# Layer 1 selects 11 columns of edges in even blocks and 10 in odd ones

## The reference

```
layer 0: ew  = (edge_attr @ W_e + b_e) as 16 x 16;  msg = x[src] . ew
         x   = layernorm(x + mean of msg over each node's edges + bias)
layer 1: A   = edge_emb[edge_type] as 16 x 16;      msg = A . x[src]
         m   = sum of msg over each node's edges
         x   = layernorm(x + GRU(m, x))
```

## Time and profile before

| what | us |
|---|---|
| median of 3 runs | 4953.85 (4951.73 to 4953.85) |
| the profiled execution | 4951.33 |
| its span | 4949.5 |
| PE busy | 4801.9 (97%) |
| DVE, ACT, POOL busy | 4057.1, 4048.1, 3499.9 |

### The profile page before, as it was taken

How to read it: one execution, slowest core, us unless ns; L and a number is a source line. 1 busy time by engine, 2 the same in 40 slices (tenths; PEclk the granted TensorE clock), 3 DMA queues, 4 the chain that set the end, 5 groups by cost and what they waited for, 6 DMA issues and landing times.

```text
span 4949.5 us, 133716 instructions
## 1 busy us (share of the span) xinstructions
PE 4801.9 (97%) x40480; PEld 4330.9 (88%) x40481; DVE 4057.1 (82%) x5504; ACT 4048.1 (82%) x5764; POOL 3499.9 (71%) x3682
## 2 busy tenths in 40 slices
PE   6999999999999999999979999999999999999997
PEld 5888888888888888888869999999999999999997
DVE  8888888888888888888867777777777777777776
ACT  7888888888888888888658888888888888888885
POOL 7777777777777777777666767676767676767674
PEclk9999999999999999999989999999999999999999
DMA  3221221221111211112221111111111111111111
GB/s 75 35 37 34 37 35 35 37 34 35 37 34 35 37 34 35 37 34 35 33 34 28 27 28 27 28 27 28 27 28 27 28 27 28 27 28 27 28 27 16
DMA packets 371461, 159.41 MB, mean 32 GB/s; under 512 B 232707, under 2 KB 370531, under 8 KB 371291
## 3 DMA queue, kind: packets, MB, share of 16 engines
q1 hardware_dynamic: 254584, 127.93, 11.4%
q0 software_dynamic: 116672, 30.10, 7.8%
q10 hardware_dynamic: 160, 0.80, 0.1%
HBM read 155.84 MB, written 2.66 MB: 32 GB/s over the span
## 4 chain that ended last, share of the span: by engine, by line
PE 84%; DVE 10%; issue 4%; DVEq 1%; POOL 1%; DMA 0%; ACT 0%; SPq 0%; POOLq 0%; ACTq 0%
PE psN L703 66%; PE psM L733 13%; DVE z L900 4%; DVE cand L871 4%; PE psTR L724 1%; PE psTR L728 1%; PE psTR L725 1%; DVE z L875 1%; PE psTR L713 1%; POOL z L461 1%; DVE grp_hot L862 0%; PE psTR L717 0%; PE psTR L714 0%; DVEq L874 0%; PE psN L816 0%
## 5 line engine op out<-in xcount | busy, mean ns | idle before, releaser
L703 PE MATMUL psN<-table_hi,pick 128*128 128x320 f32 (+1 forms) x13020 | 3879.7, 315 | 45.9 <-DVEq L843 31.2
L703 PE MATMUL psN<-table_lo,pick 128*128 128x320 f32 (+1 forms) x13020 | 3769.9, 305 | 0.0
L703 PEld LDWEIGHTS psN<-table_hi,pick 128*128 128x128 f32 x13020 | 2447.5, 188 | 224.4 <-issue 171.9
L703 PEld LDWEIGHTS psN<-table_lo,pick 128*128 128x128 f32 x13020 | 2450.2, 188 | 0.0
L461 POOL DMA_INDIRECT z<-in_x,idx x1885 | 1798.6, 954 | 658.2 <-issue 471.4
L461 POOL DMA_INDIRECT z<-h_rows,idx x1761 | 1682.9, 956 | 708.5 <-issue 475.9
L520 ACT ACTIVATE dist<-src_mod,neg_node 128x640 bf16<-128x640 uint16 (+1 forms) x2480 | 2000.0, 844 | 64.8 <-ACT pick L528 54.8
L528 ACT ACTIVATE pick<-dist,one 128x640 fp32r<-128x640 bf16 (+1 forms) x2480 | 2003.9, 846 | 23.0 <-PE psN L703 6.8
L900 DVE TENSOR_TENSOR z<-psD,z 128x2048 f32<-128x2048 f32 (+1 forms) x750 | 1367.4, 1823 | 102.2 <-issue 57.9
L871 DVE TENSOR_TENSOR cand<-psN,grp_hot 128x640 f32<-128x640 f32 x1364 | 1075.8, 789 | 434.4 <-PE psN L703 364.8
L875 DVE TENSOR_REDUCE z<-cand 128x32 f32<-128x640 f32 x1364 | 1077.6, 790 | 132.0
(11 more groups left out here) (107 smaller groups left out, 681.4 us busy)
## 6 DMA issues: line engine op xcount, KB each, us to landing
src_mod<-src_mod_rows SPq DMA_DIRECT2D x372, 160.0 KB
z<-in_x,idx POOLq DMA_INDIRECT x1885, 2.3
z<-h_rows,idx POOLq DMA_INDIRECT x1761, 2.3
eab<-in_edge_attr SPq DMA_DIRECT2D x125, 200.0 KB
src_mod<-src_mod_rows SPq DMA_DIRECT2D x124, 192.0 KB
idx<-in_src SPq DMA_DIRECT2D x250, 12.5 KB
dstb<-in_dst SPq DMA_DIRECT2D x250, 14.0 KB
grp<-src_grp SPq DMA_DIRECT2D x248, 5.5 KB, 1.6
```

Source lines behind the costliest of these rows:

```text
L703: mm = pe.matmul(rows[:, :, 0:cells.shape[2]], pick[j][:, c, at:at + P], cells, start=(i == 0 and part == 0), stop=(i == TC - 1 and part = ...
```

## The change

`H`, the number of picked columns, gets an entry for each layer and each parity: layer 0 keeps 10 and 10, layer 1 gets 11 in even and 10 in odd blocks, so odd blocks of layer 1 gather 15 columns (column 20 is the one that moves). All that hangs on `H` becomes a table by layer and parity: the halves of ScalarE's work (`HCUT`), the pairs of the selects, the waits of the gathers on picks, and the counts that semaphores are waited for, which are now sums over both parities (`ahead`, `picked_of`, `cand_of`). `TURN`, `RING`, the sizes of buffers and the host's layout stay.

```diff
-H = (10, 11)
-HM = max(H)
+H = ((10, 10), (11, 10))
+HM = max(max(h) for h in H)
-HCUT = ((0, 5, 10), (0, 5, 11))
+HCUT = [[(0, 5, h) for h in hs] for hs in H]
 TURN = (10, 12)
 RING = 4
-FIRST_S = (8, 11)
+FIRST_S = (8, 10)
-AFTER_OWN = ({3: 0, 5: 1, 6: 2, 7: 3, 8: 4, 12: 5, 13: 6}, {5: 0, 6: 1, 9: 2, 10: 3, 11: 4, 12: 5})
-AFTER_LAST = ({1: 8, 2: 9}, {1: 7, 2: 8, 3: 9, 4: 10})
+AFTER_OWN = ([{3: 0, 5: 1, 6: 2, 7: 3, 8: 4, 12: 5, 13: 6}] * 2, [{5: 0, 6: 1, 9: 2, 10: 3, 11: 4, 12: 5}, {5: 0, 6: 1, 9: 2, 10: 3, 11: 4, 13: 5}])
+AFTER_LAST = ([{1: 8, 2: 9}] * 2, [{1: 7, 2: 8, 3: 9}, {1: 7, 2: 8, 3: 9, 4: 10}])
...
+        def ahead(k, buf, r):
+            return sum(H[k]) * r + buf * H[k][0]
+        def picked_of(k, buf, r, n):
+            return ahead(k, buf, r) + H[k][1] + n
+        def cand_of(k, buf, r, n):
+            return ahead(k, buf, r) + RING + n
...
-                def held(t):
-                    if t >= RING:
-                        return t - RING
-                    return max(u for u in range(H[k]) if (u - t - TURN[k]) % RING == 0) - H[k]
-                def pick_rows(b, buf, t):
+                def pick_rows(b, buf, r, t):
...
-                    pe.wait_ge(l["cand"], RING + H[k] * b + held(t) + 1)
+                    if t >= RING:
+                        pe.wait_ge(l["cand"], cand_of(k, buf, r, t - RING + 1))
+                    else:
+                        last = max(u for u in range(H[k][1 - buf]) if (u - t - TURN[k]) % RING == 0)
+                        pe.wait_ge(l["cand"], cand_of(k, 1 - buf, r - 1 + buf, last + 1))
...
-                    for t in range(H[k]):
+                    for t in range(H[k][1 - buf]):
                         if more1:
-                            pick_rows(b + 1, 1 - buf, t)
+                            pick_rows(b + 1, 1 - buf, r + buf, t)
```

More of the change, by code:

```diff
@@ L21 @@
 PICKED = [4, 5, 6, 7, 13, 14, 21, 22, 23, 24, 20]
-H = (10, 11)
-HM = max(H)
-SCUT = [[sum(p < START[j] for p in PICKED[:h]) for j in range(NS + 1)] for h in H]
-HCUT = ((0, 5, 10), (0, 5, 11))
+H = ((10, 10), (11, 10))
+HM = max(max(h) for h in H)
+SCUT = [[[sum(p < START[j] for p in PICKED[:h]) for j in range(NS + 1)] for h in hs] for hs in H]
+HCUT = [[(0, 5, h) for h in hs] for hs in H]
 NH = 2
@@ L29 @@
 FILL = 24
-FIRST_S = (8, 11)
+FIRST_S = (8, 10)
 S_AT, T_AT, R_AT = (4, 1), (5, 3), (6, 5)
-GATHERED = [[[g for g in range(START[j], START[j + 1]) if g not in PICKED[:h]] for j in range(NS)] for h in H]
-assert all(c[-1] == h for c, h in zip(HCUT, H)) and all(2 * n % RING == 0 and n >= h for n, h in zip(TURN, H))
-PAIRS = tuple(tuple((t, min(t + 2, h)) for t in range(0, h, 2)) for h in H)
-AFTER_OWN = ({3: 0, 5: 1, 6: 2, 7: 3, 8: 4, 12: 5, 13: 6}, {5: 0, 6: 1, 9: 2, 10: 3, 11: 4, 12: 5})
-AFTER_LAST = ({1: 8, 2: 9}, {1: 7, 2: 8, 3: 9, 4: 10})
+GATHERED = [[[[g for g in range(START[j], START[j + 1]) if g not in PICKED[:h]] for j in range(NS)] for h in hs] for hs in H]
+assert all(2 * n % RING == 0 and n >= max(hs) for n, hs in zip(TURN, H))
+PAIRS = [[[(t, min(t + 2, h)) for t in range(0, h, 2)] for h in hs] for hs in H]
+AFTER_OWN = ([{3: 0, 5: 1, 6: 2, 7: 3, 8: 4, 12: 5, 13: 6}] * 2, [{5: 0, 6: 1, 9: 2, 10: 3, 11: 4, 12: 5}, {5: 0, 6: 1, 9: 2, 10: 3, 11: 4, 13: 5}])
+AFTER_LAST = ([{1: 8, 2: 9}] * 2, [{1: 7, 2: 8, 3: 9}, {1: 7, 2: 8, 3: 9, 4: 10}])
 SUB = 4
@@ L113, in build @@
         src_mod = [sb(f"src_mod{b}", [P, HM * P], U16) for b in range(2)]
-        HALF = [max(c[j + 1] - c[j] for c in HCUT) for j in range(NH)]
+        HALF = [max(c[j + 1] - c[j] for cs in HCUT for c in cs) for j in range(NH)]
         pick = [sb(f"pick{j}", [P, TC, HALF[j] * P], F32R) for j in range(NH)]
@@ L451, in body @@
                     for j in range(NS):
-                        for g in range(START[j], START[j + 1]) if whole else GATHERED[k][j]:
+                        for g in range(START[j], START[j + 1]) if whole else GATHERED[k][buf][j]:
                             if not whole:
-                                if n in AFTER_OWN[k]:
-                                    pool.wait_ge(l["picked"], H[k] * (b + 1) + AFTER_OWN[k][n] + 1)
+                                if n in AFTER_OWN[k][buf]:
+                                    pool.wait_ge(l["picked"], picked_of(k, buf, r, AFTER_OWN[k][buf][n] + 1))
                                     pool.sem_inc(s_turn)
-                                if n in AFTER_LAST[k]:
-                                    pool.wait_ge(l["picked"], H[k] * b + AFTER_LAST[k][n] + 1)
+                                if n in AFTER_LAST[k][buf]:
+                                    pool.wait_ge(l["picked"], picked_of(k, 1 - buf, r - 1 + buf, AFTER_LAST[k][buf][n] + 1))
                                     pool.sem_inc(s_turn)
@@ L684, in bank @@
                     return (TURN[k] * buf + t) % RING
-                def held(t):
+                def pick_rows(b, buf, r, t):
+                    j = max(j for j in range(NH) if HCUT[k][buf][j] <= t)
+                    at = (t - HCUT[k][buf][j]) * P
                     if t >= RING:
-                        return t - RING
-                    return max(u for u in range(H[k]) if (u - t - TURN[k]) % RING == 0) - H[k]
-                def pick_rows(b, buf, t):
-                    j = max(j for j in range(NH) if HCUT[k][j] <= t)
-                    at = (t - HCUT[k][j]) * P
-                    pe.wait_ge(l["cand"], RING + H[k] * b + held(t) + 1)
+                        pe.wait_ge(l["cand"], cand_of(k, buf, r, t - RING + 1))
+                    else:
+                        last = max(u for u in range(H[k][1 - buf]) if (u - t - TURN[k]) % RING == 0)
+                        pe.wait_ge(l["cand"], cand_of(k, 1 - buf, r - 1 + buf, last + 1))
                     for i, c in enumerate(CHUNKS):
@@ L737, in keep_busy @@
                 def keep_busy():
-                    pe.wait_ge(l["cand"], RING + H[k] * NB)
+                    pe.wait_ge(l["cand"], cand_of(k, 0, (NB - 1) // 2, H[k][0]))
                     for i in range(FILL):
@@ L760, in first_body @@
                     sum_block(0)
-                    for t in range(FIRST_S[k], H[k]):
-                        pick_rows(1, 1, t)
+                    for t in range(FIRST_S[k], H[k][1]):
+                        pick_rows(1, 1, 0, t)
                     flush_transposes(first)
@@ L873, in select @@
                         grp_hot[:, t0:t1, :].unsqueeze(2).to_broadcast([P, m, F, NG]), ALU.mult).then_inc(l["cand"], m)
-                    dve.wait_ge(l["cand"], H[k] * b + t1 + RING)
+                    dve.wait_ge(l["cand"], cand_of(k, buf, r, t1))
                     dve.tensor_reduce(xs[k][buf][:, z_pos[0]:z_pos[-1] + 1:step_pos, :], cand[:, a:a + m],
@@ L897, in outer @@
                     dve.wait_ge(l["got"][buf][j], got_of(k, buf, j, r))
-                    dve.wait_ge(l["sel"], H[k] * b + SCUT[k][j + 1])
+                    dve.wait_ge(l["sel"], ahead(k, buf, r) + SCUT[k][buf][j + 1])
                     dve.wait_ge(l["coef"], b + 1)
@@ L928, in selects @@
                         for n in pairs:
-                            select(1, 1, *PAIRS[k][n])
+                            select(1, 1, 0, *PAIRS[k][1][n])
                     if k == 0:
@@ L950, in first_body @@
                     dve.sem_inc(l["match_x"], 1)
-                    selects(*(range(2, len(PAIRS[k])) if k == 0 else range(5, len(PAIRS[k]))))
+                    selects(*range(2 if k == 0 else 5, len(PAIRS[k][1])))
                     match_block(1, 1, 0)
@@ L968, in selects @@
                             for n in pairs:
-                                select(*nxt[:2], *PAIRS[k][n])
+                                select(*nxt, *PAIRS[k][1 - buf][n])
                     outer(b, buf, r, 2)
@@ L987, in body @@
                         outer(*nxt, 1)
-                    selects(*range(3, len(PAIRS[k])))
+                    selects(*range(3, len(PAIRS[k][1 - buf])))
                     if more2:
@@ L1008, in _ @@
                 dve.sem_inc(l["free"], 1)
-                dve.sem_inc(l["picked"], 2 * H[k])
+                dve.sem_inc(l["picked"], picked_of(k, 1, 0, 0))
                 dve.sem_inc(l["pick_act"], TC * NH + 1)
-                dve.sem_inc(l["cand"], RING + H[k])
-                dve.sem_inc(l["sel"], H[k])
+                dve.sem_inc(l["cand"], cand_of(k, 1, 0, 0))
+                dve.sem_inc(l["sel"], ahead(k, 1, 0))
                 dve.sem_inc(l["hot_g"], 1)
```

18 lines of the change are left out of this document (9 added, 9 removed).

## The result

| | us |
|---|---|
| before, median of 5 runs | 4953.85 (4951.73 to 4954.96) |
| changed, median of 5 runs | 4927.37 (4925.39 to 4930.19) |
| ratio | 0.9947, 95% interval 0.9935 to 0.9958 |
| changed, the profiled execution and its span | 4930.19 and 4928.4 |

The change saves 26.5 us; 4925 was forecast, with 29.2 us. The profiled execution is the longest of the five, so the steady part is read by intervals and not by the span. Its span is 21.1 us shorter than before. From the first to the last sums of layer 1 it is 26.1 us shorter (2335.3 for 2361.3); the rest, 3.7 us ahead of the first sums and 1.2 us behind the last ones, went the other way.

What follows compares the result with a forecast made beforehand. Layer 1 was taken as nearly TensorE-bound, with VectorE's product 2 last by 0.39 us before the sums. 61 x 0.50 = 30.5, less 1.3, gives 29.2 us: 4953.85 - 29.2 = 4924.7, said as 4925; range 4908 to 4944.

Steps and rivals of the forecast that it cites:

- The ring takes the pick back: Pick 0 after an odd block still waits for `cand` of columns 8 and 9; TensorE idles 1.2 to 1.4 us.
- 0.39 us a pair from the sums that no longer wait: At the end of each even body, sums start right after pick 1, no longer after product 2: 0.39 us.
- 0.11 us from ScalarE's shorter half: Odd blocks' second half has 5 columns, not 6, so pick 5 and VectorE's chain come 0.11 us earlier.
- The gather costs nothing in the steady part: GpSimd's 15th gather in odd blocks fills its wait for a buffer: cost 0, at most 2 us in all.
- 1.3 us at the start: Block 1 of layer 1: its 15th gather delays S(1), the start of its sums, costing 1.3 us.
- the third rival: Longer idling lowers TensorE's clock from 2.4 to 1.2 GHz: 5187, or 5010 with only the sums slow; 4%.
- the pauses: Between GpSimd's gathers, 1.6 to 2.0 us over the usual gap; 0.5 us a pair added to its load.
- rival 1: The ring's wait costs nothing and VectorE stays last before the sums: gain 61.5 us, 4892; 6%.

Runs made afterwards that it cites:

- the gather alone: Kernel before, with one gather more in each odd block of layer 1 into a spare buffer, which product 2 waits for: 4955.8 us, 1.0005.
- the skipped banks: Changed kernel, but in odd blocks of layer 1 picks 2 to 9 take the bank two further on: 4892.3 us, 0.9876 of before.
- the cut at 6: Changed kernel with the skipped banks, and the 11 columns of even blocks cut 6 and 5 instead of 5 and 6: 4883.6 us, 0.9860 of before.
- the moved mask and the skipped banks: Changed kernel with the skipped banks, and VectorE's mask made behind product 2 instead of ahead of it: 4877.9 us, 0.9846 of before.
- the kernel with 10 and 10: Changed kernel with 10 picks and 15 gathers in all blocks of layer 1, `TURN = (10, 10)`: 4938.9 us, 0.9968 of before.

## Why the prediction was right

The mechanism held at each of its steps, and so did its size, 29.2 us against 26.5. The forecast for the profiled execution, 4922.1, was 8 us too low; 3 of them are the forecast's own excess, 4.9 the parts ahead of the first and behind the last sums that vary between executions. The comparison of medians is not touched by them.

- **The ring takes the pick back.** Pick 0 was to stay where it is, right behind `cand` of columns 8 and 9; it moved by 0.10 us only, as forecast by way of ScalarE (0.11), with a wait of 1.28 us (1.2 to 1.4 forecast). Undoing the cause alone gave the 0.56 us that it costs, and moving it gave a wait at the other border.
- **0.39 us a pair from the sums that no longer wait.** Measured 18.90 - 18.55 = 0.35, with ScalarE's half kept long. Of the 0.04 that is missing, some 0.03 are that picks 0 and 1 took 2.83 us behind the longer wait for 2.81, and that the sums came 0.24 us behind them for 0.23.
- **0.11 us from ScalarE's shorter half.** Measured 18.55 - 18.44 = 0.11. The chunk was not ready 0.7 us earlier, as I had it, but 0.43: a part of it is lost where ScalarE's copy of the transposed sums, between these instructions, waits for the transpose. It was enough, as the weight load had only 0.15 us to lose. Together 0.46 for the 0.50 that I took, 61 x 0.46 = 28.1 us for 30.5.
- **The gather costs nothing in the steady part.** Shown on the kernel before: 18.91 and 19.17 with it. That the same holds in the changed kernel rests on its waits, where no product waits for a gather; the run without the gather can't be read. The margin was as thin as forecast: from the start of an odd block's last gather to product 2 it is 5.2 us at the median and 3.7 at least, where the prediction needs 3.45: 1.7 and 0.2 us are left for the 2.0 and 0.3 that it had.
- **1.3 us at the start.** 1.4 in the changed kernel, 1.45 with the gather alone; by the sums of block 2 it is 1.7 and 2.2, from one execution each. 28.1 - 1.4 = 26.7, or 26.4 with 1.7, against 26.5 by the medians and 26.1 from the first to the last sums.
- **The clock.** With a wait of 1.28 us in each pair the granted clock stays at 1.00 from 2700 to 4850 us, so the third rival's condition is not met.

Some things in the prediction were wrong without harm to it. GpSimd's load was reckoned too high: the pauses, 0.5 us a pair, are still there in the changed kernel (14 from 2700 to 4700 us), but are gone in the two kernels that leave GpSimd the least slack, so the margin was 37.6 to 36.6 and not to 37.0. A pick with one issue more, by the times given, is (2.81 + 0.15) / 2 = 1.48 us and not 1.46; nothing rests on it. And rival 1, whose price was right (4892 forecast, 4892.3 measured with the skipped banks), could not come about in the changed kernel by itself.

## What to carry to other kernels

When a pass through a ring of buffers gets shorter, reckon the ring again: the wait for a buffer is met at the point where the order wraps around, and a step that was removed may have been what hid it. Put a gap of the ring where the producer has other work anyway (here the sums, 1.7 us, ahead of pick 2); that was worth more than the pick itself. And price a removed instruction by what stands behind it: if that waits for an earlier result, the instruction may have cost less than its length.

## What was not expected of the hardware

- GpSimd's pauses of 1.6 to 2.0 us between two gathers, one in about 127 us of the kernel before, did not appear when it had gathers to issue without a stop (longest idling 0.3 us over 1700 gathers). From 2700 to 4700 us there are 16 of them before and 8 to 17 in the kernels whose pair of blocks takes 37.05 us or more, but 2 in that with the cut at 6 (36.94) and none in that with the moved mask and the skipped banks (36.85). What makes them was not found.
- An instruction of 0.38 us on VectorE between two dependent ones cost 0.17 us.
- At waits of 1.28 us once a pair TensorE's granted clock stayed at 1.00; in the kernel with 10 and 10, whose sums waited up to 2.5 us for product 2, it was 0.98 over the stretch, between its two levels of 1.2 and 2.4 GHz on average.
- On one chip five kernels of this case took about a third longer (6464 to 6712 us), in the four profiles with TensorE idling ahead of single matmuls for no releaser that the profile shows, and a granted clock of 0.89 to 0.95 from 5000 to 6000 us. The cause is open.
